# Last layer's dense attention: two query tiles weighed together in products of 256 columns

## What is computed

```python
qkv = jnp.einsum('bth,hnd->bntd', X, wqkv)            # 8 heads of 64
Q, K, V = jnp.split(qkv, 3, axis=-1)
Q, K = _rope(Q, pos, N_ROT, BASE), _rope(K, pos, N_ROT, BASE)
att = jnp.einsum('bnqd,bnkd->bnqk', Q, K) / jnp.sqrt(HP)
att = jnp.where(causal, att, -jnp.inf)                # key <= query
AV = jnp.einsum('bnqk,bnkd->bnqd', jax.nn.softmax(att, axis=-1), V)
dense = AV.transpose(0, 2, 1, 3).reshape(b, t, NH_D * HP) @ wo
```

## Time and profile before

| | |
|---|---|
| median of 3 executions | 629.09 us (629.04, 629.09, 634.01) |
| profiled execution, its own time | 627.68 us |
| span in it, first to last instruction | 625.9 us |
| PE busy | 531.9 us, 85% of the span |
| DVE, ACT, POOL busy | 337.0, 228.6, 133.1 us |
| mean granted clock of PE | 0.935 |

### The profile page before, as it was taken

The page is one execution under the profiler, slowest core; times in us unless marked ns, Lnnn a source line. Parts: engine busy times, 40 slices in busy tenths (PEclk is TensorE's granted clock), DMA queues, the critical chain, the costliest instruction groups (busy, mean ns, idle before and its releaser), DMA issues.

```text
span 625.9 us, 7679 instructions
## 1 busy us (share of the span) xinstructions
PE 531.9 (85%) x2992; PEld 357.9 (57%) x2992; DVE 337.0 (54%) x676; ACT 228.6 (37%) x452; POOL 133.1 (21%) x111
## 2 busy tenths in 40 slices
PE   5689999957899987979987997986868888997886
PEld 3468788827367553458863774762335455455553
DVE  1356677532542355368735563554598466537661
ACT  2444445322031113323333335323454344425651
POOL 7621221203050001234310002103311311303200
PEclk9889999965799977879999999989897997999999
DMA  9300000016000000000000001000000000000000
GB/s 366 124 1 2 2 0 1 1 32 227 1 1 0 2 0 1 0 0 2 2 1 0 2 5 63 1 0 2 0 1 1 1 1 0 2 18 2 1 1 17
DMA packets 3573, 13.76 MB, mean 22 GB/s; under 512 B 785, under 2 KB 1042, under 8 KB 3026
## 3 DMA queue, kind: packets, MB, share of 16 engines
q1 hardware_dynamic: 3538, 13.27, 5.6%
HBM read 12.75 MB, written 0.52 MB: 21 GB/s over the span
## 4 chain that ended last, share of the span: by engine, by line
PE 59%; DVE 23%; issue 7%; ACT 6%; POOL 5%; DMA 1%; SPq 0%; DVEq 0%; POOLq 0%; ACTq 0%
PE PS L446 49%; PE PS L552 5%; DVE den L1700 3%; POOL rstd L1900 2%; DVE mx L1427 2%; DVE wmoe L1420 2%; PE PS L888 2%; PE PS L464 1%; DVE mx L1435 1%; DVE mxd L1718 1%; ACT wmoe L1264 1%; POOL wmoe L1929 1%; DVE yb L1741 1%; DVE wlate L1439 1%; DVE m L1740 1%
## 5 line engine op out<-in xcount | busy, mean ns | idle before, releaser
L446 PE MATMUL PS<-keys,PTB 128*128 128x308 f32 x224 | 71.2, 447 | 8.8 <-DVE PT L1500 1.9
L446 PEld LDWEIGHTS PS<-va,PT 128*128 128x128 f32 (+1 forms) x480 | 58.6, 192 | 6.9 <-DVE PT L1500 2.5
L446 PE MATMUL PS<-va,PT 128*128 128x72 f32 (+2 forms) x480 | 58.3, 273 | 1.7 <-DVE PT L1500 1.6
L446 PEld LDWEIGHTS PS<-keys,PTB 128*128 128x128 f32 x224 | 39.1, 194 | 33.2 <-issue 13.6
L1941 POOL TENSOR_TENSOR wmoe<-wmoe,cst 128x1024 f32<-128x1024 f32 (+1 forms) x8 | 17.7, 2210 | 118.4 <-ACT wmoe L1238 118.4
L1900 POOL TENSOR_TENSOR rstd<-veps,mhalf 128x4 f32<-128x4 f32 x16 | 16.5, 1041 | 112.7 <-DVE veps L1356 112.7
L1929 POOL TENSOR_TENSOR wmoe<-wmoe,mx 128x616 f32<-128x616 f32 (+1 forms) x24 | 25.0, 1044 | 60.3 <-DVE mx L1429 34.3
L1929 POOL TENSOR_TENSOR wlate<-wlate,mx 128x616 f32<-128x616 f32 x16 | 19.4, 1216 | 72.2 <-DVE mx L1435 72.2
L1264 ACT ACTIVATE wmoe<-PS,mxd 128x512 f32<-128x512 f32 (+3 forms) x64 | 33.0, 525 | 4.1 <-DVE mxd L1718 4.0
L1276 ACT COPY PTB<-PS 128x768 f32<-128x768 f32 (+1 forms) x24 | 20.8, 869 | 32.7 <-PE PS L888 32.6
L1145 ACT ACTIVATE wmoe<-wmoe 128x616 f32<-128x616 f32 (+1 forms) x32 | 18.4, 586 | 37.5 <-POOL wmoe L1929 37.4
(11 more groups left out here) (309 smaller groups left out, 1082.3 us busy)
## 6 DMA issues: line engine op xcount, KB each, us to landing
wmoe<-w_dram SPq DMA_DIRECT2D x2, 2048.0 KB, 11.9
wa<-wa_dram SPq DMA_DIRECT2D x4, 256.0 KB, 6.7
wlate<-ew_dram SPq DMA_DIRECT2D x2, 512.0 KB, 5.7
wd<-wd_dram SPq DMA_DIRECT2D x1, 1024.0 KB, 9.4
wlate<-wm_dram SPq DMA_DIRECT2D x1, 1024.0 KB, 4.7
cst<-const_dram SPq DMA_DIRECT2D x1, 736.0 KB, 8.2
cst<-const_dram SPq DMA_DIRECT2D x1, 688.5 KB, 5.0
ctxr<-ctx_dram SPq DMA_DIRECT2D x1, 616.0 KB, 5.9
```

What stands on the lines that cost most here:

```text
L446: return nc.tensor.matmul(o, l, r, start=start, stop=stop, skip_group_check=True)
```

## The change

The weighing of the first turn (tile 3) is no longer done by itself. Its transposed weights and those of the second turn (tile 2) go to one buffer `PTW`, in which for each key block k the 128 columns of tile 2 and the 128 columns of tile 3 stand side by side. `weigh` does nothing for i = 0; for i = 1 it takes both tiles in one product of 256 columns for k = 0, 1, 2, and tile 3 alone for k = 3. Third turns have a buffer of their own, `PTN`, in tile `pool_iota`. ACT's copies wait for other counts of `d_weighed`, which now rises by 4 for a pair instead of 6, and the wait for `d_taken` moves with the first weighing of a pair.

```diff
-        PTR = [PTB[:, 2 * r:2 * r + 2] for r in range(2)]
+        PTW = PTB[:, 0:4].rearrange("p (z a) t -> p z (a t)", z=2).rearrange("p z (k c q) -> p z k c q", k=4, c=2)
+        PTN = pool_iota[:, 64:64 + 768].rearrange("p (z a) -> p z a", z=2)
...
                     r, i = divmod(n, 3)
                     b, p = divmod(r, 4)
+                    if i == 0:
+                        return
                     pe.wait_ge(S("d_turned"), n + 1)
                     pe.wait_ge(S("d_v_placed"), TB * (b + 1))
-                    if i == 0 and r > 0:
+                    if i == 1 and r > 0:
                         pe.wait_ge(S("d_taken"), r)
 
-                    parts = [(3, 4, 0, k, k * 128) for k in range(4)] if i == 0 else \
-                        [(2, 3, 0, k, k * 128) for k in range(3)] if i == 1 else [(0, 2, 0, 0, 0), (1, 2, 0, 1, 256)]
-                    for m, (t0, t1, _, k, at) in enumerate(parts):
+                    wide_ = [(2, 4, k, PTW[:, :, k, 0:2, :].rearrange("p z c q -> p z (c q)")) for k in range(3)] + \
+                        [(3, 4, 3, PTW[:, :, 3, 1, :])]
+                    narrow = [(0, 2, 0, PTN[:, :, 0:256]), (1, 2, 1, PTN[:, :, 256:384])]
+                    parts = wide_ if i == 1 else narrow
+                    for m, (t0, t1, k, src) in enumerate(parts):
...
-                                      PTR[n % 2][:, z, at:at + (t1 - t0) * 128], start=(m == 0), stop=(m == len(parts) - 1))
+                                      src[:, z, :], start=(m == 0), stop=(m == len(parts) - 1))
...
                     act.wait_ge(S("d_groups"), n + 1)
-                    if n >= 2:
-                        act.wait_ge(S("d_weighed"), 2 * (n - 1))
-                    width = 128 * sum(t + 1 for t in TURNS[n % 3])
-                    nc.scalar.copy(PTR[n % 2][:, :, 0:width], PS[:, 4:6, 0:width]).then_inc(S("d_turned"), 1)
+                    r, i = divmod(n, 3)
+                    if r > 0 and i != 1:
+                        act.wait_ge(S("d_weighed"), 4 * r - (2 if i == 0 else 0))
+                    if i == 2:
+                        dst, width = PTN[:, :, 0:384], 384
+                    else:
+                        dst, width = PTW[:, :, 0:4 - i, 1 - i, :], 512 - 128 * i
+                    nc.scalar.copy(dst, PS[:, 4:6, 0:width] if i == 2 else
+                                   PS[:, 4:6, 0:width].rearrange("p z (k q) -> p z k q", q=128)).then_inc(S("d_turned"), 1)
...
-                    act.wait_ge(S("d_weighed"), 6 * (r + 1))
+                    act.wait_ge(S("d_weighed"), 4 * (r + 1))
```

## The result

| | before | after |
|---|---|---|
| median of 4 executions | 629.93 us (629.04 to 634.01) | 640.12 us (638.09 to 641.82) |
| profiled execution, its own time | 627.68 us | 641.82 us |
| span, mean granted clock | 625.9 us, 0.935 | 640.0 us, 0.909 |
| `scores(0)` to the end | 189.1 us | 199.2 us |

The account below looks back on a forecast made before the run. The last layer's path was taken to pass between PE, ACT's exponentials and DVE. Pair terms summed to +1.1 us, plus 1.7 for one more clock fall: +2.8, 631.9 us, range 626.8 to 635.2.

Parts of the forecast that it names:

- Columns are the price: PE's weighing: 128 columns in both halves cost 0.105 us, a product by itself next to nothing; wide weighing 1.72 us.
- the back-to-back gaps: Skill's figures for PE's products: wide passes would save 0.4 us a pair; as a rival, 627.5 us, chance 0.04.
- The ledger by pairs: Path cost, pairs 0 to 7: 0, +0.84, +0.07, -0.40, 0, +0.84, -0.78, +0.55; sum +1.1 us.
- The layout is free: ACT's copies into the new buffers, writing runs of 128 columns with gaps, were taken to cost 0 extra.
- one more fall for 1.7 us: PE's clock falls once more, at turn 17 or 23, costing 1.7 us; chance of this forecast 0.38.
- "Slower" rival: Lower clock at the long pauses in pairs 2, 5 and 7: +6.2 us, 635.3 us; chance 0.16.
- The pause at turn 17: Pair 5: PE's pause ahead of this turn grows by 1.03 us, from 1.79 to 2.8 us.
- Those of pair 2: PE's 0.79 us wait for DVE in this pair grows to about 1.8 us.
- turn 23: Pair 7: PE's pause ahead of this turn grows from 1.48 to 2.5 us.
- Pair 3: No wait swallows the first weighing's gain of 1.03 us; 0.63 us of the second is added: -0.40 us.
- the slack at `swap(4)`: Pair 2: DVE starts 0.77 us after the product is ready, leaving +0.07 of 0.84 us.
- PE's waits for the exponentials: PE's waits for ACT ahead of turns grow from 7.0 us by about 4.
- If the clock falls elsewhere: Named as one sign, for PE's clock, that would make the prediction wrong; no size given.

Follow-up runs that it names:

- e2: Changed kernel with the second turn's weighing done in 14 products of 128 columns instead of wide ones; 641.43 us, ratio 1.020.
- e3: Kernel before with only the new buffers and waits, each weighing in its old place and size; 629.38 us, ratio 1.001.
- e14: Kernel before with the new buffers and the regrouped weighing in pair 3 alone; 634.59 us, ratio 1.009.
- e5: Kernel before with the new buffers and the regrouped weighing in pairs 3 and 6 only; 632.51 us, ratio 1.005.
- e4: Changed kernel with the weighing of query tile 3 left out everywhere, so its output lacks that part; 629.78 us, ratio 1.002.
- e1: Changed kernel with each pair's eight removed products put back in their old place and overwritten by the wide ones; 634.37 us, ratio 1.006.
- e16: Kernel before with the new buffers and the regrouped weighing in pair 2 only; 633.52 us, ratio 1.009.
- e13: Changed kernel with six PE pauses filled with constant products, the 5.7 us pause and pair 3 among them; 634.36 us, ratio 1.006.
- e9: Kernel before with constant products added in five PE pauses, nothing else changed; 625.72 us, ratio 0.992.
- e10: Changed kernel without query tile 3's weighing, with four PE pauses filled with constant products; 630.02 us, ratio 0.999.
- e8: Changed kernel with constant products added in four PE pauses; 637.55 us, ratio 1.010.

## Why the prediction was wrong

- **Columns are the price** was right. The wide weighing takes 1.74 us (1.72 predicted), and in e2 28 records of 128 columns take 1.75 in its place. So the saving that the back-to-back gaps of the Trainium skill ("TensorE: Matmul & The Clock Gate", section "Back-to-back issue gap") would give wide products is not there.
- **The ledger by pairs** was right in its places: +0.86, +0.09, 0, -0.82 where +0.84, +0.07, 0, -0.78 were said. The layout is free (e3).
- **The step that failed is the clock's.** The text had one more fall for 1.7 us. The period at the 5.7 us pause came in two pieces; three new ones came, at 507, 596 and 623 us, and the one at 531 was twice as long, together 20.4 us more at the lower level. In the table of lateness they are the excess over ledger and missed waits: -1.22 + 2.59 + 2.98 + 1.60 + 1.49 = 7.4 us (2.98 is pair 3's 3.34 + 0.40, less 0.76 for a missed wait), 0.37 us for each us at the lower level. This is what is left over, put down to the clock; it isn't measured by itself. I had priced 0.25 (1.7 of 6.7). The "Slower" rival had this mechanism at 0.16 and with 6.2 us; its three places were right (pairs 2, 5, 7), a fourth was missing.
- **All executions, and not only the profiled ones**, give the clock a part of the same size or a little less. Over the 89 of before, 1 us more at the lower level goes with 0.32 us more time (0.26 without the slowest seven). The four of after have on average 20.5 us more of it (113.6 against 93.2) and take 10.3 us more: by these rates the clock has 5 to 7 us of them. Ledger and missed waits have 2.6; the rest, 1 to 2.5 us, has no place in the account. This is an estimate, as after's low times (102 to 120 us) lie mostly beyond those of before (81 to 109).
- **The pause at turn 17** didn't become one of 2.8 us. It came in two pieces, 0.87 us for DVE at 591.17 and 1.91 us ahead of turn 17: the transposes (L950) behind the removed weighing now wait for DVE to read bank 7 (L1802). The prediction had added the whole 1.03 us to one wait. The clock fell at 596 all the same. Those of pair 2 (1.67 us) and turn 23 (2.51) were as forecast (1.8 and 2.5).
- **Pair 3 was the worst reading.** "Around the first weighing PE is busy 6.48 of 6.70 us, so there is no wait to swallow the gain" took that as a gain. The rows said more: this was the stretch at the end of which the clock came back, and the work to be removed was part of what kept PE busy in it. The prediction said "if that period ends at the same moment as now" and priced no other case. In after, e14 and e5 it lasts 13.6 us; it is the largest single item, +3.34 instead of -0.40. e4 shows that the weighing isn't all: with an earlier fall the period was short without it.
- **A wait that the weighing covered** (missed): the transposes of the filler `turn3` at 532.86 wait 0.76 us for ACT (L1300), which reads bank 7 out between two fillers. The weighing stood between them. Of the 1.91 us only 1.07 came back (lateness 7.11 to 6.04).
- **DVE behind POOL** (missed): the slack at `swap(4)` took up 0.71 of 0.84 us for PE, but `prepare(4)` and POOL's `rope` behind it stay 7.1 us late. DVE's subtraction L1807 (64 x 512, two inputs) takes 2.08 us instead of 1.39; both times it ends 0.55 us after POOL's (518.89 and 519.44; 526.00 and 526.55). ACT's copy `xc`, for which `spread(2)` waits, comes behind it. What e3 and e1 show:

```profile
522.02 1.36 DVE L1810 TENSOR_TENSOR yb<-yb,sps 64x512 f32<-64x512 f32 x1
```

```profile
522.13 2.09 DVE L1806 TENSOR_TENSOR yb<-yb,sps 64x512 f32<-64x512 f32 x1
```

  e3 (first) has pair 2's weighing narrow and in its old place, e1 has it wide: 1.36 and 2.09 us. The page "SBUF — State Buffer" of the Trainium skill, section "SBUF: two separate sides", has the rule: a DVE operation with two inputs in SBUF and a GpSimd operation that reads SBUF exclude each other, and the later one waits for the whole of the earlier. The trace agrees, and so does the reduction L1806 with its one input, which takes its 0.68 us beside POOL's operation (at 523.76).
- **PE's waits for the exponentials** were to grow from 7.0 us by about 4. They grew by 1.7, as part of PE's pauses went into slower work:

```profile
PE PS L889 <- ACT wmoe L1269: 8.7, 6, 2.5
```

- **The first 4.1 us** of the profile's difference were chance: the period of 13.6 us at 418 stands ahead of all changed code. Of the 16 profiled executions that can be read, seven have it, e3's among them, of a kernel that takes 629.4; in the others it lasts 3.4 us. How many of the unprofiled ones have it is not known.
- "If the clock falls elsewhere" was named as what would make the prediction wrong. It fell in the pairs with the long pauses, as the slower rival had it, and stayed low in pair 3, which no case had. The new 5 in the PEclk line is that of pair 3, at 528 to 544 us, and none stands after 584.

What stays open: what exactly decides where a fall comes and how long it lasts. The wait of 1.79 us ahead of turn 17 brought none in before and e16, and one in e14, with the same instructions around it. And why most executions of e13 have a lower clock than the profiled one.

## What to carry to other kernels

Work of PE ahead of a wait has two prices: what it takes, and what the pause without it does to the clock. Before removing or moving such work, look at the granted clock by stretch, and ask of each pause that will grow whether a fall follows, and of each low period which work ends it. A few products of constants in the longest pauses of a kernel are cheap to try; here they brought 0.8% in the kernel before, but in the changed kernel the clock still fell in most executions. One profiled execution is a sample: compare its mean clock with those of the other executions before building on where the clock fell. And when an instruction is taken from between two users of one buffer, the read-out that it covered becomes a wait.

## What the hardware showed

- 0.28 us (before to e9, profiles), 0.32 us (89 executions of before) and 0.37 us (before to after, by what was left over) lost for each us at the lower clock, and nothing for 10.2 us of it from e4 to e10.
- A low period lasted 6.8 us with PE busy 6.48 of 6.70 us in it, and 13.6 us in six kernels in which the weighing at its start was gone (after, e2, e5, e8, e10, e14), in e14 with PE busy 12.52 of 13.70; in e4, without the weighing, it lasted 6.8 us with PE busy 5.84 of 6.60.
- DVE's 64 x 512 subtraction took 0.68 us alone (at 591.77 of after) and 1.36 to 2.09 us with POOL's `rope` under way, ending 0.55 us after it.
